# A state-space layer's y clipped and gated in eight pieces of 512 tokens instead of four of 1024

## The chip, the cores and the metric

The program runs on one core of one Trainium2 chip. The metric is the device time of one launch in microseconds. Three runs of the kernel before gave 1256.93, 1259.4 and 1264.48 us, so the median is 1259.4 us. Within a core the engines named here work side by side and wait for one another through semaphores: PE (TensorE, matrix products), DVE (VectorE), ACT (ScalarE), POOL (GpSimd) and SP, which issues DMAs.

## The reference, cut to what matters

The whole program is four transformer-like layers, each a mixer and a feed-forward part. The change is in the mixer of layer 0, a Mamba-style state-space model. Its core, with 2 batches of 1024 tokens, 256 inner channels and 16 states, is:

```
h = dA * h + (dt_t * u_t)[..., None] * B_t[:, None, :]   # one step of the scan
y = jnp.einsum('bdn,bn->bd', h, C_t)
...
y = jnp.transpose(ys, (1, 0, 2)) + x * D
y = _bound(y)                       # clip to 0..1
gate = jax.nn.silu(z)
y = _bound(y * gate)
return jnp.einsum('bld,ed->ble', y, W_out)
```

After it come the residual addition, a layer norm, a modulation and the feed-forward part of layer 0, whose inputs and hidden values are rounded to FP4 in blocks of 16 (scale by the block's largest magnitude). `Bm`, `Cm`, `dt` and `z` are computed ahead of the scan and aren't touched.

(The shapes: `B` in the kernel is 2, `S` 1024, `NTOK` 2048.)

## The kernel before, in words

Everything in layer 0 is written out by hand: five functions, one for each engine's queue, and counts of semaphores that tie them together. No scheduler reorders anything. A queue is worked off in order, so a wait holds all that stands behind it on its engine.

The 256 channels are two halves of 128 partitions (`e` = 0, 1; `ET` = 2). A batch's 1024 tokens are two pieces of `CH` = 512 (`hf` = 0, 1; `CPB` = 2). The scan therefore has the steps (batch `b`, state `n`, `e`, `hf`), with `hf` running fastest: 64 steps for a batch (`per_b`), 128 in all. For each step q: PE spreads the row of B over the partitions (`b_row`, L565), DVE multiplies it by dt*u (`multiply`, L712; every fourth step on POOL instead, L909), ACT makes the decay (L852), DVE scans (L750), POOL multiplies by the row of C (L919), and PE adds the product into one of four PSUM banks (L599), bank 4 + 2e + hf. The last state closes the four banks in the order (e0, first tokens), (e0, last tokens), (e1, first tokens), (e1, last tokens). The semaphore `acc` counts these sums. PE and POOL trail the scans: DVE reaches the end of batch b at iteration q = p + `LAG` with `LAG` = 3.

There DVE (`vector_scan`, L754 to L766) clips the batch out of PSUM into `u`, one instruction for each channel half (L758, 128x1024), then multiplies by the gate `gz` in place (L765, 128x1024). `y_step` counts these four. PE's `outputs(b, hf)` multiplies a piece of 512 tokens by W_out (L578): for each of 4 tiles of 128 tokens, both halves e are summed, 8 products, which the trace shows as 16 matmul records. Both calls wait for all of the batch's y: `YSTEP * (b + 1)`.

After batch 0 DVE rounds a weight to FP4 (`quantise_weight(2)`, L216 to L246), and goes on into batch 1's scan with two residual additions among it (`add_outputs`, L719, with the statistics L145 and L149 behind it). PE must put `outputs(0, 0)` ahead of the first row, `skip_product` and sum of batch 1. After batch 1 DVE normalises the tokens of batch 0 (L168, eight instructions), does the additions of batch 1's two pieces, each behind PE's outputs, and goes into the feed-forward part: a copy of transposed weights (L1002), six products (L1008), and `quantise_h` (L216 to L246). POOL modulates the normalised tokens of batch 0 (L1067, L1069) and computes the deviations of batch 1's pieces (L160, L162). PE, after its outputs, transposes the feed-forward weights (L1078, L1081) and runs six filler products (`keep_busy`, L1126) half-way through each end of the FP4 work.

Of the kernel before, what the change touches and what calls it, by code (L numbers as in the profile page):

```python
# [6 lines left out]
ALU = mybir.AluOpType  # L7
# [9 lines left out]
B, S = 2, 1024  # L17
# [3 lines left out]
CH = 512  # L21
NCH = NTOK // CH
TPC = CH // P
CPB = S // CH
# [4 lines left out]
ET = DI // P  # L29
# [46 lines left out]
def _program(nc, A, out, top):  # L76
# [6 lines left out]
    pe, dv, ac, gp, sp = nc.tensor, nc.vector, nc.scalar, nc.gpsimd, nc.sync  # L83
    ps = top.enter_context(nc.psum_tensor("ps", [P, 8, CH], F32))
# [6 lines left out]
    gate = sb("gate", [P, NL, 2, B, D])  # L91
# [278 lines left out]
    def layer0_mixer(ctx):  # L370
# [3 lines left out]
        gz = sb("gz", [P, ET, NTOK], ctx=ctx)  # L374
        u = sb("u", [P, ET, NTOK], ctx=ctx)
# [27 lines left out]
                                                  sem("acc"))  # L403
        y_step, y_mm = sem("y_step"), sem("y_mm")
        TAPS, SKIP, SEL, NEGA = KC, KC + ET, KC + ET + 1, KC + ET + 2
        ROWS, YSTEP = 5, 2 * ET

        DT, GZ = (ET * (NCH - 1), ET * NCH + 2), ET * NCH
        SILU_1 = float(1.0 / (1.0 + np.exp(-1.0)))
# [20 lines left out]
        def y_bank(b, hf):  # L430

            return 0 if b == B - 1 and hf else 3

        def by_gpsimd(q):
            return q % per_n == per_n - 1
# [97 lines left out]
        def tensor_scan():  # L533
# [6 lines left out]
            def skip_product(b, e, hf):  # L540

                t0 = b * S + hf * CH
                pe.wait_ge(dt_out, ET * NCH + 2)
                pe.wait_ge(l0_const, SKIP)
                if b > 0:
                    pe.wait_ge(y_step, YSTEP * (b - 1) + ET)
                pe.matmul(ps[:, 4 + e * CPB + hf, :], skip[:, e, :], u[:, e, t0:t0 + CH], start=True, stop=False)

            def c_row(k, i):
# [18 lines left out]
            def outputs(b, hf, bank3):  # L568

                bank = y_bank(b, hf)  # L570
                pe.wait_ge(y_step, YSTEP * (b + 1))
                pe.wait_ge(l0_wog, B)
                if bank == 3:
                    pe.wait_ge(*bank3)
                for t in range(TPC):
                    t0 = b * S + hf * CH + t * P
                    for e in range(ET):
                        i = pe.matmul(ps[:, bank, t * P:(t + 1) * P], u[:, e, t0:t0 + P], wog[:, b, e, :],  # L578
                                      start=e == 0, stop=e == ET - 1)
                i.then_inc(y_mm, 1)  # L580
                return x_new, b * CPB + hf + 1
# [5 lines left out]
            for q in range(NQ + LAG):  # L587
# [5 lines left out]
                p = q - LAG  # L593
# [112 lines left out]
        def vector_scan():  # L706
# [20 lines left out]
            for q in range(NQ + LAG):  # L727
                if q in add_at:
                    add_outputs(0, add_at[q])
                if q in REST_AT:  # L730
                    rest_bc(1, REST_AT[q])
                if q == 24:
                    rows_dt(1)
                if q + 1 < NQ and not by_gpsimd(q + 1):
                    multiply(q + 1)
                if q < NQ:
                    b, n, e, hf = steps[q]
                    k = q // per_n
                    if by_gpsimd(q):
                        dv.wait_ge(gp_inputs, k + 1)  # L740
                        operands = ps[:, q % NB_, :], gin[:, k % 2, :]
                    else:
                        dv.wait_ge(inputs, nth(q) + 1)
                        operands = dA[:, q % SL, :], ps[:, q % NB_, :]
                    dv.wait_ge(decayed, q + 1)
                    if q >= SL:
                        dv.wait_ge(times_c, q - SL + 1)
                    if hf:
                        dv.wait_ge(scanned, q)
                    dv.tensor_tensor_scan(hs[:, q % SL, :], *operands,  # L750
                                          hs[:, (q - 1) % SL, CH - 1:CH] if hf else 0.0,
                                          ALU.mult, ALU.add).then_inc(scanned, 1)
                p = q - LAG
                if p >= 0 and p % per_b == per_b - 1:  # L754
                    b = p // per_b
                    dv.wait_ge(acc, p + 1)
                    for e in range(ET):
                        dv.tensor_scalar(u[:, e, b * S:(b + 1) * S],  # L758
                                         ps[:, 4 + e * CPB:4 + (e + 1) * CPB, :].rearrange("p a n -> p (a n)"),
                                         0.0, 1.0, ALU.max, ALU.min).then_inc(y_step, 1)  # L760
                    dv.wait_ge(xz_z, GZ + ET * (b + 1))
                    for e in range(ET):
                        dst = u[:, e, b * S:(b + 1) * S]
                        dv.wait_ge(y_step, YSTEP * b + e + 1)
                        dv.scalar_tensor_tensor(dst, gz[:, e, b * S:(b + 1) * S], SILU_1, dst,  # L765
                                                ALU.min, ALU.mult).then_inc(y_step, 1)  # L766
                    if b == 0:
                        quantise_weight(2)
                    else:
                        for c in range(b * CPB):  # L770
                            normalise(1, c)
                        for hf in range(CPB):
                            add_outputs(b, hf)
# [2327 lines left out]
```

## Time and profile before

| what | value |
|---|---|
| median of 3 runs | 1259.4 us (1256.93 to 1264.48) |
| span of the profiled execution | 1233.1 us |
| what lies around the span, against the median | 26.3 us |
| PE busy | 908.0 us, 74% |
| DVE busy | 899.4 us, 73% |
| ACT busy | 581.5 us, 47% |
| POOL busy | 548.8 us, 45% |
| mean granted TensorE clock | 0.865 |

The profile holds no device time of its own for the execution it shows. The 26.3 us are the median less the span, and stand here for what lies before the first and after the last instruction. Layer 0's scan runs from about 80 to 316 us, its feed-forward part from there to about 425 us. In the rows a time is the start in us from the span's first instruction. One row can hold several instructions of a kind (x2), and its duration then covers them all. Where a bracket ends the row, the engine was idle for that long before it, until the named engine's instruction.

### The profile page before, as it was taken

The numbers are of one execution on the slowest core, as the hardware profiler recorded it, in microseconds if no ns is written. First come the engines' busy times: TensorE is split into PE (matmuls) and PEld (weight loads), VectorE is DVE, ScalarE is ACT, GpSimd is POOL, SyncE is SP. The second block draws the span as 40 slices with busy tenths as digits, with TensorE's granted clock in tenths as the row PEclk, the third lists the DMA queues.
The fourth block names the chain that finished last, engine by engine and source line by source line (L and its number), as shares of the span: only waits on it lengthen the run. The fifth ranks groups of instructions, "written<-read, shape, count | busy, mean of one in ns | idle before, by whom it ended". The sixth has DMA issues, their size and how long they took to land.

```text
span 1233.1 us, 18682 instructions
## 1 busy us (share of the span) xinstructions
PE 908.0 (74%) x5207; PEld 528.8 (43%) x5207; DVE 899.4 (73%) x1692; ACT 581.5 (47%) x1232; POOL 548.8 (45%) x553
## 2 busy tenths in 40 slices
PE   6977787888666676668888888858996481258992
PEld 3423233333335544212223322348996251156882
DVE  6679999999899737787888875185553689984323
ACT  3477664666033242506776667624543481023332
POOL 2058996999410132501111211225643587335753
PEclk9879898999878897959999999869998595568997
DMA  9000000000000210320110110061111000001113
GB/s 300 1 1 1 1 0 1 1 0 1 1 0 1 86 51 0 100 66 17 28 32 24 28 28 2 1 241 40 45 35 53 38 1 0 0 35 40 48 40 115
DMA packets 28016, 46.30 MB, mean 38 GB/s; under 512 B 8720, under 2 KB 16408, under 8 KB 26896
## 3 DMA queue, kind: packets, MB, share of 16 engines
q1 hardware_dynamic: 22672, 34.67, 8.7%
q0 software_dynamic: 4096, 8.35, 2.3%
q10 hardware_dynamic: 1152, 2.10, 0.5%
q8 instruction: 48, 0.79, 0.3%
q14 instruction: 48, 0.39, 0.1%
HBM read 34.46 MB, written 12.58 MB: 38 GB/s over the span
## 4 chain that ended last, share of the span: by engine, by line
PE 43%; DVE 29%; issue 11%; ACT 7%; POOL 5%; DMA 3%; SPq 1%; DVEq 0%; ACTq 0%; POOLq 0%
PE ps L2791 10%; PE ps L2800 6%; PE ps L1814 5%; PE ps L1796 4%; POOL sb_gs L919 4%; DVE sb_hs L750 3%; DVE sb_l_mxp L1928 2%; PE ps L1741 2%; DVE sb_xn L168 2%; DVE sb_stats L145 2%; ACT sb_l_rc L2221 1%; PE ps L1749 1%; PE ps L599 1%; ACT sb_l_pT L1871 1%; PE ps L478 1%
## 5 line engine op out<-in xcount | busy, mean ns | idle before, releaser
L1928 DVE TENSOR_REDUCE sb_l_mxp<-ps 128x2 f32<-128x1024 f32 (+3 forms) x152 | 171.3, 1163 | 40.1 <-PE ps L1741 38.8
L919 POOL TENSOR_TENSOR sb_gs<-sb_hs,sb_xp 128x512 f32<-128x512 f32 x128 | 163.2, 1295 | 23.7 <-DVE sb_hs L750 21.9
L1871 ACT ACTIVATE sb_l_pT<-ps 128x512 f32<-128x512 f32 (+3 forms) x256 | 111.4, 521 | 76.3 <-PE ps L1796 75.0
L599 PE MATMUL ps<-sb_gs,sb_ident 128*128 128x512 f32 x256 | 133.9, 605 | 1.0 <-POOL sb_gs L919 0.8
L2791 PE MATMUL ps<-sb_hT,sb_f_shared 128*128 x936 | 123.8, 283 | 6.5 <-issue 2.4
L2791 PEld LDWEIGHTS ps<-sb_hT,sb_f_shared 128*128 128x128 f32 x936 | 113.3, 196 | 14.9 <-issue 14.9
L1796 PE MATMUL ps<-sb_l_qk 51*128 51x512 bf16 (+3 forms) x384 | 88.6, 334 | 18.9 <-ACT sb_l_pT L1871 8.1
L2861 DVE SCALAR_TENSOR_TENSOR sb_f_rows<-ps,sb_f_mask,sb_f_rows 128x128 f32 x78 | 27.3, 351 | 91.1 <-PE ps L2800 61.3
L865 ACT ACTIVATE sb_xp<-ps 128x512 f32<-128x512 f32 x96 | 57.1, 595 | 73.2 <-POOL sb_gs L919 41.6
L2889 POOL DMA_INDIRECT moe_y<-sb_f_rows,sb_f_rowi x64 | 64.1, 1002 | 61.3 <-DVE sb_f_rows L2861 49.4
L2830 ACT ACTIVATE sb_f_hid<-ps 128x512 f32<-128x512 f32 x78 | 46.6, 597 | 90.7 <-PE ps L2791 90.7
L2800 PE MATMUL ps<-sb_sw_f_out,sb_f_hid 128*128 x624 | 83.5, 277 | 0.7 <-DVE sb_f_hid L2850 0.6
L2884 POOL DMA_INDIRECT sb_f_inq<-moe_h,sb_f_toki x64 | 62.9, 983 | 43.7 <-DVE sb_f_rowi L2662 16.3
L750 DVE TENSOR_TENSOR_SCAN sb_hs<-sb_dA,ps 128x512 f32<-128x512 f32 x64 | 76.8, 1200 | 0.1
L2800 PEld LDWEIGHTS ps<-sb_sw_f_out,sb_f_hid 128*128 128x128 f32 x624 | 75.8, 192 | 1.2 <-issue 1.1
L160 POOL TENSOR_SCALAR sb_rstd<-sb_meanvar 128x4 f32<-128x4 f32 x32 | 9.9, 311 | 146.9 <-DVE sb_meanvar L149 146.8
L1741 PE MATMUL ps<-sb_l_qk 48*128 48x128 bf16 (+3 forms) x576 | 68.3, 297 | 8.6 <-DVE sb_l_mxp L1928 8.5
L1796 PEld LDWEIGHTS ps<-sb_l_qk 51*128 51x128 bf16 x384 | 25.5, 94 | 113.4 <-issue 107.9
L2017 POOL TENSOR_SCALAR_AFFINE_SELECT sb_l_raw<-sb_l_raw 128x512 f32<-128x512 f32 x24 | 15.2, 634 | 130.7 <-ACT sb_l_raw L1871 130.6
L2017 POOL TENSOR_SCALAR_AFFINE_SELECT sb_l_pT<-sb_l_pT 128x512 f32<-128x512 f32 x40 | 25.4, 635 | 95.2 <-ACT sb_l_pT L1871 95.1
L712 DVE TENSOR_TENSOR ps<-sb_mod_space,ps 128x512 f32<-128x512 f32 x96 | 64.5, 672 | 4.1 <-PE ps L565 4.1
L852 ACT ACTIVATE sb_dA<-sb_dt,sb_negA 128x512 f32<-128x512 f32 x96 | 65.5, 712 | 0.8 <-DVE sb_hs L750 0.8
(394 smaller groups left out, 2047.1 us busy)
## 6 DMA issues: line engine op xcount, KB each, us to landing
sb_sw_f_in<-w_f_in SPq DMA_DIRECT2D x2, 2048.0 KB, 10.3
sb_sw_f_out<-w_f_out SPq DMA_DIRECT2D x2, 2048.0 KB, 13.9
sb_l_qk<-spill SPq DMA_DIRECT2D x112, 32.0 KB
spill<-sb_l_parts SPq DMA_DIRECT2D x12, 256.0 KB, 2.9
moe_y<-c_f_zero SPq DMA_DIRECT2D x1, 2048.0 KB, 9.5
sb_sw_f_up<-w_f_up SPq DMA_DIRECT2D x1, 2048.0 KB, 12.0
moe_h<-sb_f_rows SPq DMA_DIRECT2D x8, 256.0 KB, 5.2
sb_f_rows<-moe_y SPq DMA_DIRECT2D x8, 256.0 KB, 6.0
```

Source lines behind the costliest of these rows:

```text
L599: pe.matmul(ps[:, 4 + e * CPB + hf, :], ident[:], gs[:, p % SL, :], start=False, stop=n == DS - 1).then_inc(acc, 1)
L712: dv.tensor_tensor(ps[:, q % NB_, :], dtu[:, e, t0:t0 + CH], ps[:, q % NB_, :], ALU.mult).then_inc(inputs, 1)
L750: dv.tensor_tensor_scan(hs[:, q % SL, :], *operands, hs[:, (q - 1) % SL, CH - 1:CH] if hf else 0.0, ALU.mult, ALU.add).then_inc(scanned, 1)
L852: ac.activation(dst, dt[:, e, t0:t0 + CH], ACT.Exp, scale=negA[:, e, n:n + 1]).then_inc(decayed, 1)
L919: gp.tensor_tensor(gs[:, q % SL, :], hs[:, q % SL, :], cs[:, k % 2, hf * CH:(hf + 1) * CH], ALU.mult).then_inc(times_c, 1)
L1741: m = pe.matmul(ps[:, b0 + half, col:col + width], qs[i][rows, slot, t * P:(t + 1) * P], ks[i][rows, slot, key:key + width], start=start, ...
L1796: pe.matmul(ps[:, bank[n_sc], 0:width], ks[i][rows, h // 2, kt * P:(kt + 1) * P], qs[i][rows, h // 2, q0:q0 + width], start=True, stop=Tru ...
L1871: ac.activation(pT[e % 3][:, h, 0:width], ps[:, bank[n_bank], 0:width], ACT.Exp, scale=L2_SCALE).then_inc(exped, 1)
L1928: dv.tensor_reduce(dst, src, AX_X, ALU.max).then_inc(max_out, 1)
L2791: m = pe.matmul(ps[:, 2 * (i % 2) + n, fs], own[:, i % 2, n, fs], xr[:, bass.ds(r, 1), :], start=True, stop=True)
L2800: m = pe.matmul(ps[:, Y_BANK[i % 2], 0:D], hid[:, i % NBUF, f * P:(f + 1) * P], w_out[:, bass.ds(e, 1), f, :], start=f == 0, stop=f == FT - 1)
L2889: gp.indirect_dma_start(ysum, bass.IndirectOffsetOnAxis(ap=row_i[:, k:k + 1], axis=0), y_all[:, k, :], None, bounds_check=2 * NTOK - 1, oo ...
```

## The change

The clip and the gate are issued as eight instructions of 128x512 instead of four of 128x1024. Their order is a table: the clips of channel half 0 (first, last tokens), the gates of half 0, then for half 1 clip and gate of the first tokens, clip and gate of the last tokens. Each clip waits for the last sum of its own bank, each gate for its own clip. `outputs(b, hf)` waits for the gate of channel half 1 and its own tokens, which is the sixth of the eight for `hf` = 0 and the eighth for `hf` = 1. The first product into each bank of batch 1 (`skip_product`) waits for the clip of that bank. The wait for `gz` stands ahead of the clips. The line numbers below this place grow by 6 or more.

```diff
-        ROWS, YSTEP = 5, 2 * ET
+        ROWS, YSTEP = 5, 2 * ET * CPB
...
+        Y_ORDER = ([("clip", 0, hf) for hf in range(CPB)] + [("gate", 0, hf) for hf in range(CPB)]
+                   + [(what, e, hf) for hf in range(CPB) for e in range(1, ET) for what in ("clip", "gate")])
+
+        def y_at(b, what, e, hf):
+            return y_step, YSTEP * b + Y_ORDER.index((what, e, hf)) + 1
...
                 if b > 0:
-                    pe.wait_ge(y_step, YSTEP * (b - 1) + ET)
+                    pe.wait_ge(*y_at(b - 1, "clip", e, hf))
...
-                pe.wait_ge(y_step, YSTEP * (b + 1))
+                pe.wait_ge(*y_at(b, "gate", ET - 1, hf))
...
-                    dv.wait_ge(acc, p + 1)
-                    for e in range(ET):
-                        dv.tensor_scalar(u[:, e, b * S:(b + 1) * S],
-                                         ps[:, 4 + e * CPB:4 + (e + 1) * CPB, :].rearrange("p a n -> p (a n)"),
-                                         0.0, 1.0, ALU.max, ALU.min).then_inc(y_step, 1)
                     dv.wait_ge(xz_z, GZ + ET * (b + 1))
-                    for e in range(ET):
-                        dst = u[:, e, b * S:(b + 1) * S]
-                        dv.wait_ge(y_step, YSTEP * b + e + 1)
-                        dv.scalar_tensor_tensor(dst, gz[:, e, b * S:(b + 1) * S], SILU_1, dst,
-                                                ALU.min, ALU.mult).then_inc(y_step, 1)
+                    for what, e, hf in Y_ORDER:
+                        t0 = b * S + hf * CH
+                        dst = u[:, e, t0:t0 + CH]
+                        if what == "clip":
+                            dv.wait_ge(acc, p + 1 - per_n + e * CPB + hf + 1)
+                            dv.tensor_scalar(dst, ps[:, 4 + e * CPB + hf, :], 0.0, 1.0,
+                                             ALU.max, ALU.min).then_inc(y_step, 1)
+                        else:
+                            dv.wait_ge(*y_at(b, "clip", e, hf))
+                            dv.scalar_tensor_tensor(dst, gz[:, e, t0:t0 + CH], SILU_1, dst,
+                                                    ALU.min, ALU.mult).then_inc(y_step, 1)
```

DVE's queue at the end of batch 1, before: the last scan, then the clips of whole halves out of the banks `ps`, the gates, and the first normalisation. The brackets name the semaphores that an instruction waits for.

```order
L750 SCALAR_TENSOR_TENSOR sb_hs<-ps,sb_hs,sb_xp 128x512 [waits times_c,scanned,decayed,gp_inputs]
L758 TENSOR_SCALAR sb_u<-ps 128x1024 [waits acc]
L758 TENSOR_SCALAR sb_u<-ps 128x1024
L765 SCALAR_TENSOR_TENSOR sb_u<-sb_gz,sb_u 128x1024 [waits y_step,xz_z]
L765 SCALAR_TENSOR_TENSOR sb_u<-sb_gz,sb_u 128x1024 [waits y_step]
L168 TENSOR_SCALAR sb_xn<-sb_x,sb_meanvar,sb_rstd 128x128 [waits ln_rstd]
```

The same place of the changed kernel:

```order
L756 SCALAR_TENSOR_TENSOR sb_hs<-ps,sb_hs,sb_xp 128x512 [waits times_c,scanned,decayed,gp_inputs]
L768 TENSOR_SCALAR sb_u<-ps 128x512 [waits acc,xz_z]
L768 TENSOR_SCALAR sb_u<-ps 128x512 [waits acc]
L772 SCALAR_TENSOR_TENSOR sb_u<-sb_gz,sb_u 128x512 [waits y_step] x2
L768 TENSOR_SCALAR sb_u<-ps 128x512 [waits acc]
L772 SCALAR_TENSOR_TENSOR sb_u<-sb_gz,sb_u 128x512 [waits y_step]
L768 TENSOR_SCALAR sb_u<-ps 128x512 [waits acc]
L772 SCALAR_TENSOR_TENSOR sb_u<-sb_gz,sb_u 128x512 [waits y_step]
L168 TENSOR_SCALAR sb_xn<-sb_x,sb_meanvar,sb_rstd 128x128 [waits ln_rstd]
```

The four instructions have become eight, and every clip has its own wait for `acc`. Nothing else on DVE has changed its place. The end of batch 0 has the same eight, between the scan of step 66 and `quantise_weight(2)`.

PE's queue is the same before and after, but for the counts it waits for. It is shown at the end of batch 0, where three things of batch 1 stand behind the first outputs (L578): the row of B (L565), the product that opens a bank (L547) and the first sum (L599). Then come the outputs of the last tokens.

```order
L599 MATMUL ps<-sb_gs,sb_ident 128x512 [waits times_c]
L578 MATMUL ps<-sb_wog,sb_u 128x128 [waits crow,l0_wog,y_step]
L578 MATMUL ps<-sb_wog,sb_u 128x128 x7
L565 MATMUL ps<-sb_bc,sb_sel 128x512 [waits scanned,rows_step]
L547 MATMUL ps<-sb_u,sb_skip 128x512 [waits y_step,l0_const,dt_out]
L599 MATMUL ps<-sb_gs,sb_ident 128x512 [waits times_c]
L578 MATMUL ps<-sb_wog,sb_u 128x128 [waits x_new,l0_wog,y_step]
L578 MATMUL ps<-sb_wog,sb_u 128x128 x7
```

No row moves here. What moves is the time at which `y_step` lets the first L578 go.

## Rows read from the trace of the kernel before

**Rows 1.** Busy time by stretch: start:end, length, PE, PEld, DVE, ACT, POOL, clock, DMA, GB/s.
```profile
218.00:308.00 90.00, 73.40 (x195) 28.35 (x194) 87.92 (x97) 57.96 (x97) 86.84 (x73) 0.98 0.00 1
329.80:417.80 88.00, 54.82 (x212) 37.29 (x213) 84.92 (x135) 23.63 (x65) 11.21 (x12) 0.78 0.00 1
```

**Rows 2.** DVE in order of time, end of batch 0: start, us, instruction.
```profile
199.47 1.19 DVE L750 TENSOR_TENSOR_SCAN sb_hs<-sb_dA,ps 128x512 f32<-128x512 f32 x1
201.19 2.35 DVE L758 TENSOR_SCALAR sb_u<-ps 128x1024 f32<-128x1024 f32 x2 [0.52 <-PE ps L599]
203.46 2.35 DVE L765 SCALAR_TENSOR_TENSOR sb_u<-sb_gz,sb_u 128x1024 f32<-128x1024 f32 x2
205.73 0.51 DVE L216 TENSOR_REDUCE sb_f0w_small<-sb_sw_f_dn 128x22 f32<-128x352 f32 x1
...
209.90 0.68 DVE L719 TENSOR_TENSOR sb_x<-sb_x,ps 128x512 f32<-128x512 f32 x1
...
212.40 1.27 DVE L750 TENSOR_TENSOR_SCAN sb_hs<-ps,sb_hs,sb_xp 128x512 f32<-128x512 f32 x1
214.21 0.69 DVE L719 TENSOR_TENSOR sb_x<-sb_x,ps 128x512 f32<-128x512 f32 x1 [0.54 <-PE ps L578]
```

**Rows 3.** DVE in order of time, end of batch 1 and start of the feed-forward part.
```profile
307.60 0.67 DVE L712 TENSOR_TENSOR ps<-sb_mod_space,ps 128x512 f32<-128x512 f32 x1
308.18 1.21 DVE L750 TENSOR_TENSOR_SCAN sb_hs<-sb_dA,ps 128x512 f32<-128x512 f32 x1
...
312.41 1.28 DVE L750 TENSOR_TENSOR_SCAN sb_hs<-ps,sb_hs,sb_xp 128x512 f32<-128x512 f32 x1
316.36 2.35 DVE L758 TENSOR_SCALAR sb_u<-ps 128x1024 f32<-128x1024 f32 x2 [2.67 <-PE ps L599]
318.63 2.35 DVE L765 SCALAR_TENSOR_TENSOR sb_u<-sb_gz,sb_u 128x1024 f32<-128x1024 f32 x2
320.90 2.13 DVE L168 TENSOR_SCALAR sb_xn<-sb_x,sb_meanvar,sb_rstd 128x128 f32<-128x128 f32 x8
324.86 0.69 DVE L719 TENSOR_TENSOR sb_x<-sb_x,ps 128x512 f32<-128x512 f32 x1 [1.82 <-PE ps L578]
...
327.84 0.69 DVE L719 TENSOR_TENSOR sb_x<-sb_x,ps 128x512 f32<-128x512 f32 x1 [0.97 <-PE ps L578]
...
329.76 0.86 DVE L1002 COPY sb_f_wguT<-ps 128x704 f32<-128x704 f32 x1
```

**Rows 4.** PE in order of time, around both ends.
```profile
212.22 1.95 PE L578 MATMUL ps<-sb_wog,sb_u 128*128 128x128 f32 x16
...
311.54 4.79 PE L599 MATMUL ps<-sb_gs,sb_ident 128*128 128x512 f32 x8 [0.75 <-POOL sb_gs L919]
321.04 6.76 PE L578 MATMUL ps<-sb_wog,sb_u 128*128 128x128 f32 x32 [4.71 <-DVE sb_u L765]
```

**Rows 5.** One form on DVE, 128x512 with two inputs in SBUF (L624).
```profile
L624 DVE SCALAR_TENSOR_TENSOR sb_u<-sb_xp,sb_sw_l_vec,sb_u x12: 750/752/753, 22.2 to 35.9; 128x512 f32<-128x512 f32 x12
```

**Rows 6.** POOL in order of time, at both ends and in the feed-forward part.
```profile
198.61 3.73 POOL L919 TENSOR_TENSOR sb_gs<-sb_hs,sb_xp 128x512 f32<-128x512 f32 x3
...
310.22 4.93 POOL L919 TENSOR_TENSOR sb_gs<-sb_hs,sb_xp 128x512 f32<-128x512 f32 x4
...
328.59 1.04 POOL L162 TENSOR_TENSOR sb_rstd<-sb_rstd,sb_half 128x4 f32<-128x4 f32 x1
...
341.74 1.28 POOL L1067 TENSOR_TENSOR sb_hT<-sb_xn,sb_mod 128x512 f32<-128x512 f32 x1
```

**Rows 7.** DVE, the same step of the FP4 work, twice.
```profile
333.25 0.69 DVE L228 TENSOR_TENSOR sb_f_tmp<-sb_hT,sb_f_small 128x512 f32<-128x512 f32 x1
...
341.87 1.70 DVE L228 TENSOR_TENSOR sb_f_tmp<-sb_hT,sb_f_small 128x512 f32<-128x512 f32 x1
```

**Rows 8.** Busy time by stretch around the ends, and later.
```profile
201.20:205.80 4.60, 0.00 (x0) 0.00 (x0) 4.60 (x5) 0.94 (x2) 1.14 (x1) 0.84 0.00 0
205.80:211.20 5.40, 5.34 (x19) 4.53 (x20) 5.05 (x15) 0.00 (x0) 0.00 (x0) 0.51 0.00 0
316.30:321.00 4.70, 0.03 (x1) 0.00 (x0) 4.64 (x5) 0.00 (x0) 0.00 (x0) 0.93 0.01 2
321.00:327.30 6.30, 6.26 (x29) 6.26 (x30) 3.97 (x17) 0.00 (x0) 4.03 (x4) 0.51 0.00 0
415.00:419.30 4.30, 4.25 (x19) 3.83 (x20) 2.80 (x13) 1.50 (x6) 1.26 (x2) 0.50 0.00 0
421.80:460.00 38.20, 28.15 (x132) 18.56 (x130) 15.51 (x56) 19.07 (x28) 13.47 (x12) 1.00 0.28 110
```

## The prediction

> **What bounds the kernel now.** I read the views in this order: busy time by stretch, to see which engine has no room near the change. Then DVE in order of time at the two places where a batch ends, then PE and POOL at the same places, and last the clock. In the body of the scan DVE is busy for 87.92 of 90 us and POOL for 86.84 [rows 1]. So anything that DVE saves or loses at the end of batch 0 is passed on unshortened. In the feed-forward part behind the scan DVE is busy for 84.92 of 88 us [rows 1], and the reader should see that it is the engine with the least room up to 416 us. A microsecond gained by DVE at 329.76 is a microsecond gained at the end of layer 0's feed-forward part.
>
> At the end of batch 0 DVE finishes its scan at 199.47 + 1.19 = 200.66, and starts to clip at 201.19, behind PE's last sum. It then works without a hole until 213.67, and waits 0.54 us for PE's second outputs [rows 2]. At the end of batch 1 there is more to see. DVE's last scan ends at 312.41 + 1.28 = 313.69. The four last sums are one chain on PE from 311.54 to 316.33 [rows 4], paced by POOL, whose four products run from 310.22 to 315.15 [rows 6]. DVE idles 2.67 us and clips at 316.36 when the last is in [rows 3]. Its gates end at 320.98, PE starts the outputs at 321.04 after 4.71 us without work [rows 4], and DVE, having normalised, waits for them 1.82 us and then 0.97 us [rows 3]. These three holes, 5.46 us, are what could be won there. The second pair is PE's time: 32 matmul records in 6.76 us [rows 4] at a granted clock of 0.51 [rows 8], the lower level of 1.2 GHz. The same 16 records took 1.95 us at full clock [rows 4].
>
> **The change part by part.**
>
> The eight pieces. A whole clip or gate starts 2.27/2 = 1.135 us after the one before it (201.19, 203.46, 205.73) [rows 2]. A 128x512 instruction on DVE starts 0.58 us before the next (307.60 to 308.18 [rows 3]), while its own duration is 0.67. Eight at 0.58 are 4.64 us against 4.54 before. Two gates stand right behind the clip they wait for (half 1), so each pays a full duration and a little, about 0.14 more: 4.64 + 0.28 = 4.92, taken as 4.95. Bounds: 4.64 from below, and 8 x 0.75 = 6.0 from above, if every piece costs what L624 costs [rows 5]. I take 4.95, nearest to the row of the same shape without a scalar from memory. The cost is +0.4 us a batch.
>
> POOL beside the gates. The gates read two tensors from SBUF, and now start while POOL still multiplies. The trace has such a meeting: the same DVE step took 0.69 us alone, and 1.70 us when it began at 341.87 within POOL's 341.74 to 343.02 [rows 6, 7]. It ended at 343.57, which is POOL's end plus about its own time, so it was held until POOL had finished. By these rows a gate that starts while POOL works is held to the end of that POOL instruction. At batch 0 the first gate would start at about 201.8, and POOL works to 202.34 [rows 6]: +0.5 us. At batch 1 it would start at about 314.8, and POOL's last product ends at 315.15: +0.35 us. The bounds are 0 and these values. I take them in full. The Trainium skill's page "SBUF — State Buffer", section "SBUF: two separate sides", has this as a lock: a DVE instruction with two SBUF inputs and a GpSimd instruction that reads SBUF exclude each other for a whole instruction. By the page the two delays are what the rows give, and without it the sum would be 0.85 us better.
>
> Batch 0 then: the clips start 0.59 us earlier (200.60, as a follower starts 0.08 before the end of the one ahead), the pieces take 0.41 more, the lock 0.5. DVE is 0.3 us later at L216. PE's first outputs wait for the sixth piece, at about 200.60 + 4 x 0.58 + 0.5 + 0.72 + 0.67 = 204.8, and start 1.0 us earlier than 205.86 even at the low clock. So the row, the opening product and the sum of batch 1 that stand behind them on PE are earlier too, and the second outputs are bound by DVE's first addition instead (209.90 [rows 2] + 0.3 + 0.69 = 210.9). They take 1.95 us, and are ready at 212.9, before DVE's scan ends at 213.97. The 0.54 us hole goes. Batch 0: -0.2 us.
>
> Batch 1: the first clip starts at 313.61 right behind the scan (its bank's sum, the first of four in 4.79 us [rows 4], is over by 312.8). The clip of (half 1, first tokens) comes at 313.61 + 2.32 + 0.35 = 316.28, its sum, the third, ends a sum and a wait, 1.2 us, before 316.33. The last clip's sum ends at 316.33, before DVE asks for it at 317.6. No clip waits. The gates end with DVE free at 313.61 + 4.95 + 0.35 = 318.91, against 320.90: -2.0 us. PE may start its outputs at the end of the sixth piece, 317.7, instead of 321.04, after only 1.4 us without work. In the scan PE has holes of that kind all the time at a clock of 0.98 [rows 1]. The clock fell before, late in a hole of 4.7 us (mean 0.93 in 316.3 to 321.0 [rows 8]). So I take the full clock: 16 records in 1.95 us, the first outputs ready at 319.7, the second at 321.6. DVE normalises until 320.97, adds at once, and comes to the second addition 2.0 us later, at 323.0. Both holes go: -1.82 - 0.97 = -2.79. Batch 1: -4.8 us at L1002, which would start at 325.0.
>
> What is late next. The weights' transposes on PE end near 323, before DVE asks. POOL's modulations follow the normalisation and end near 326.4. Only then do its two deviations come, each with an instruction of 1.04 us [rows 6], and they now lie beside DVE's FP4 steps from 327, where before they lay beside additions and copies that read PSUM. If they hold DVE once, that costs up to 0.8 us. The trace doesn't show this pair. Bounds 0 and 0.8, and I take the middle, 0.4, having no nearer row.
>
> Behind that everything is shifted together up to 416 us, where the end of layer 0 and all later stages follow. Sum: -0.2 - 4.8 + 0.4 = -4.6 us. The profiled execution has a span of 1233.1 us, and 26.3 us lie between that and the median: 1228.5 + 26.3 = 1254.8 us (-0.37%).
>
> **The rivals.**
>
> Rival 1, the clock stays low for the outputs. At batch 0 it had fallen by 205.8, and was at 0.51 until 211.2 [rows 8]. If PE's outputs of batch 1 run at the lower level, 32 records take about 6.8 us. From 317.7 the first 16 end at 321.5 and the second at 324.9, so 0.55 + 1.4 = 2.0 us of DVE's holes stay. Gain 2.6 us, time 1256.8. Against it stands the short hole of 1.4 us.
>
> Rival 2, more than the sum. If POOL doesn't hold the gates or the FP4 steps, 0.85 + 0.4 us come back. The chain at the end of the feed-forward part (415.0 to 419.3 at a clock of 0.50, PE busy for 4.25 of 4.3 us [rows 8]) can fall at full clock once it comes at another moment, worth up to 4.3/2 = 2.1 us. Together 3.4 more: 1251.4. For it: the clock's spells are not tied to the kernel's stages. Against: the rows of POOL and DVE are plain.
>
> Rival 3, slower: low-clock spells move into stages that PE bounds. From 421.8 to 460 PE is busy 28.15 of 38.2 us at a clock of 1.00 [rows 8]. A spell like the one of 321 to 327.3 there would cost 6.3 x 0.74 / 2 = 2.3 us. Everything behind 318 us comes 4.8 us earlier, so where spells fall is dealt anew. Two more such spells take the gain back, and from there it is slower. With four it is 1254.8 + 9.2 = 1264.0. For it: the mean clock is 0.865, so much is at stake. Against: the low spells of today can go as well as come, and four more of one sign are unlikely.
>
> Rival 4, the gain doesn't last: the feed-forward part turns out to wait for PE or POOL, whose work doesn't come earlier. Then only batch 0's 0.2 us stays, 1259.2. DVE's 84.92 of 88 us [rows 1] speaks against it.
>
> **How the numbers follow.** The forecast gets 0.50 (own range 1252.5 to 1257), rival 1 0.12, rival 2 0.22, rival 3 0.12, rival 4 0.04. Half a per cent of 1259.4 is 6.3 us, about what a measurement can tell from no change. So faster means below 1253.1: rival 2 and a tail of the forecast, 0.30. Slower means above 1265.7, the upper tail of rival 3, 0.07. The rest, 0.63, is within. The range goes from 1248.5, a little beyond rival 2, to 1260.5, which takes in rivals 1 and 4 and a part of rival 3. The likeliest time is faster than before, but by less than can be told with certainty.
>
> **What would show each step.** Right: eight rows of 128x512 at each end, about 0.67 us each with starts 0.58 apart. The first gate longer than the second by about 0.5 us at batch 0 and 0.35 at batch 1. No idle time before L768 at batch 1 (2.67 before). L584, the outputs, after a hole of about 1.4 us at clock 1.0, 16 records in 1.95 us. No hole before either L725 at batch 1. The copy of the weights (L1002 before) 4.8 + 0.2 = 5.0 us earlier. Wrong: a clip that still waits for PE, pieces near 0.75 us, or outputs at 0.5. The forecast as a whole is wrong if the last gates of layer 0 are 5 us earlier and the span isn't.

## The result and the profile after

Over 20 runs of each kernel the changed one had a median of 1258.74 us, against 1263.2 us of the kernel before. The medians are 4.5 us apart. The ratio is 0.9953, with a 95% interval of 0.9935 to 0.9971: 5.9 us less, 3.7 to 8.2. One run of the changed kernel took 1407.42 us at a granted clock of 0.62 and is left out of the ratio. So the changed kernel is faster, by a little less than half a per cent, the outcome to which the prediction gave 0.63. Two later measurements beside the experiments gave 0.9944 (0.9923 to 0.9966) and 0.9959 (0.9941 to 0.9977). The forecast was -4.6 us, 1254.8 us, with a range of 1248.5 to 1260.5.

The profiled execution of the changed kernel has a span of 1257.2 us and took 1258.5 us. So only 1.3 us lie around this span, and not the 26.3 us that the first table and the forecast took for it. The first experiment below says what those were.

DVE at the end of batch 0, to be read against [rows 2]; the columns are start, duration, engine, line, operation and operands.

```profile
198.84 1.19 DVE L756 TENSOR_TENSOR_SCAN sb_hs<-sb_dA,ps 128x512 f32<-128x512 f32 x1
199.96 1.26 DVE L768 TENSOR_SCALAR sb_u<-ps 128x512 f32<-128x512 f32 x2
201.13 1.72 DVE L772 SCALAR_TENSOR_TENSOR sb_u<-sb_gz,sb_u 128x512 f32<-128x512 f32 x2
202.78 0.68 DVE L768 TENSOR_SCALAR sb_u<-ps 128x512 f32<-128x512 f32 x1
203.49 0.69 DVE L772 SCALAR_TENSOR_TENSOR sb_u<-sb_gz,sb_u 128x512 f32<-128x512 f32 x1
...
205.43 0.51 DVE L216 TENSOR_REDUCE sb_f0w_small<-sb_sw_f_dn 128x22 f32<-128x352 f32 x1
...
213.29 0.66 DVE L725 TENSOR_TENSOR sb_x<-sb_x,ps 128x512 f32<-128x512 f32 x1
```

The scan of step 66 started 0.63 us earlier than in the first profile, for a cause ahead of the change, so ways are compared and not clock times. From the start of that scan to the start of the second addition it is 213.29 - 198.84 = 14.45 us, against 14.74. The addition has no idle time before it now. Batch 0 gives 0.29 us.

DVE at the end of batch 1, against [rows 3]:

```profile
311.47 1.28 DVE L756 TENSOR_TENSOR_SCAN sb_hs<-ps,sb_hs,sb_xp 128x512 f32<-128x512 f32 x1
312.67 1.26 DVE L768 TENSOR_SCALAR sb_u<-ps 128x512 f32<-128x512 f32 x2
313.85 1.50 DVE L772 SCALAR_TENSOR_TENSOR sb_u<-sb_gz,sb_u 128x512 f32<-128x512 f32 x2
315.28 0.68 DVE L768 TENSOR_SCALAR sb_u<-ps 128x512 f32<-128x512 f32 x1
315.99 0.69 DVE L772 SCALAR_TENSOR_TENSOR sb_u<-sb_gz,sb_u 128x512 f32<-128x512 f32 x1
316.60 0.68 DVE L768 TENSOR_SCALAR sb_u<-ps 128x512 f32<-128x512 f32 x1
317.31 0.69 DVE L772 SCALAR_TENSOR_TENSOR sb_u<-sb_gz,sb_u 128x512 f32<-128x512 f32 x1
317.92 2.14 DVE L168 TENSOR_SCALAR sb_xn<-sb_x,sb_meanvar,sb_rstd 128x128 f32<-128x128 f32 x8
319.98 0.68 DVE L725 TENSOR_TENSOR sb_x<-sb_x,ps 128x512 f32<-128x512 f32 x1
...
321.89 0.66 DVE L725 TENSOR_TENSOR sb_x<-sb_x,ps 128x512 f32<-128x512 f32 x1
...
323.79 0.86 DVE L1009 COPY sb_f_wguT<-ps 128x704 f32<-128x704 f32 x1
```

No row has idle time before it: 2.67, 1.82 and 0.97 us are gone. From the start of the last scan to the copy of the weights it is 12.32 us, against 17.35. That is 5.03 us, the whole of batch 1's gain. I call this way "the batch 1 way" below, and the 14.45 us "the batch 0 way".

PE at the same place, against [rows 4]:

```profile
310.59 4.79 PE L605 MATMUL ps<-sb_gs,sb_ident 128*128 128x512 f32 x8 [0.75 <-POOL sb_gs L926]
316.73 3.84 PE L584 MATMUL ps<-sb_wog,sb_u 128*128 128x128 f32 x32 [1.35 <-DVE sb_u L772]
```

The 32 records take 3.84 us instead of 6.76, behind a hole of 1.35 instead of 4.71. Busy time by stretch says why (length, PE, PEld, DVE, ACT, POOL, then the granted clock):

```profile
316.70:320.60 3.90, 3.87 (x34) 3.87 (x35) 3.87 (x11) 0.00 (x0) 0.46 (x1) 1.00 0.01 2
...
411.10:417.60 6.50, 4.99 (x35) 3.92 (x33) 3.76 (x18) 2.97 (x8) 2.43 (x5) 1.00 0.17 35
```

The clock is 1.00 in the outputs, the level of 2.4 GHz, where it was 0.51. The second row is the tail of the feed-forward part. There the last piece's chain ran at 1.00, where [rows 8] show 0.50 for most of it. DVE's rows there:

```profile
410.83 1.09 DVE L168 TENSOR_SCALAR sb_xn<-sb_x,sb_meanvar,sb_rstd 128x128 f32<-128x128 f32 x4
414.12 0.69 DVE L1040 TENSOR_TENSOR sb_x<-sb_x,ps 128x512 f32<-128x512 f32 x1 [2.20 <-PE ps L1125]
...
417.60 2.13 DVE L168 TENSOR_SCALAR sb_xn<-sb_x,sb_meanvar,sb_rstd 128x128 f32<-128x128 f32 x4 [0.47 <-POOL sb_rstd L162]
```

DVE waits 2.20 us for PE there. The same view of the kernel before has a longer wait at this addition:

```profile
421.75 0.69 DVE L1033 TENSOR_TENSOR sb_x<-sb_x,ps 128x512 f32<-128x512 f32 x1 [3.89 <-PE ps L1118]
```

So another 1.7 us were gained at a place that the change doesn't touch. There the granted clock was at 0.50 from 409.1 to 419.4 us before, and from 401.5 to 408.3 us in the changed kernel, ahead of this chain. This 1.7 us does not come each time: it was there in two of three profiles of the changed kernel and in three other kernels' profiles, one of which has batch 1 as before. In the third profile of the changed kernel the wait was 3.79 us.

POOL and DVE in the feed-forward part, where 0.4 us of holding was forecast. First POOL, then DVE:

```profile
325.60 1.07 POOL L162 TENSOR_TENSOR sb_rstd<-sb_rstd,sb_half 128x4 f32<-128x4 f32 x1
...
326.93 1.04 POOL L162 TENSOR_TENSOR sb_rstd<-sb_rstd,sb_half 128x4 f32<-128x4 f32 x1
```

```profile
326.46 0.18 DVE L219 TENSOR_SCALAR sb_f_small<-sb_f_small 128x32 f32<-128x32 f32 x1
...
327.27 0.69 DVE L228 TENSOR_TENSOR sb_f_tmp<-sb_hT,sb_f_small 128x512 f32<-128x512 f32 x1
```

Both DVE steps began within a POOL instruction of about 1.04 us and took what they take alone. The second is the very step (L228) that took 1.70 us beside a 128x512 instruction of POOL in [rows 7]. Nothing was held. The kernel before has the same kind of pair, further on in the feed-forward part, POOL first and then DVE:

```profile
401.45 1.04 POOL L162 TENSOR_TENSOR sb_rstd<-sb_rstd,sb_half 128x4 f32<-128x4 f32 x1
```

```profile
401.97 1.61 DVE L1028 TENSOR_TENSOR sb_f_hh<-sb_f_sg 128x1408 f32<-128x1408 f32 x1
```

This DVE step too has two inputs in SBUF. It began half-way through the POOL instruction and took 1.61 us, like its three repetitions elsewhere (1.59 to 1.62).

### The profile page after: what moved, and what is told of

It is laid out like the page before. It is cut to its first block, busy times and chain, and to the rows that moved or that the text cites. A ratio compares the mean times of both kernels' runs of the same rounds, so it can differ in the third digit from the quotient of the medians.

```text
span 1257.2 us, 18690 instructions
## 1 busy us (share of the span) xinstructions
PE 915.5 (73%) x5207; PEld 533.2 (42%) x5207; DVE 899.7 (72%) x1700; ACT 578.6 (46%) x1232; POOL 547.4 (44%) x553
## 4 chain that ended last, share of the span: by engine, by line
PE 39%; DVE 30%; issue 11%; ACT 8%; POOL 5%; DMA 3%; another core or an unknown queue 2%; SPq 1%; DVEq 0%; ACTq 0%; POOLq 0%
PE ps L2798 9%; PE ps L2807 5%; PE ps L1821 5%; PE ps L1803 4%; DVE sb_hs L756 3%; POOL sb_gs L926 3%; DVE sb_l_mxp L1935 2%; PE ps L1748 2%; DVE sb_xn L168 2%; DVE sb_stats L145 2%; ACT sb_l_rc L2228 1%; PE ps L1756 1%; ACT sb_l_pT L1878 1%; DVE ps L718 1%
## 5 line engine op out<-in xcount | busy, mean ns | idle before, releaser
L2798 PE MATMUL ps<-sb_hT,sb_f_shared 128*128 x936 | 127.5, 288 | 13.6 <-ACT sb_f_shared L2815 6.8
L2798 PEld LDWEIGHTS ps<-sb_hT,sb_f_shared 128*128 128x128 f32 x936 | 116.6, 200 | 22.2 <-issue 22.2
L2807 PE MATMUL ps<-sb_sw_f_out,sb_f_hid 128*128 x624 | 86.3, 283 | 14.0 <-ACT sb_f_hid L2837 9.3
L2807 PEld LDWEIGHTS ps<-sb_sw_f_out,sb_f_hid 128*128 128x128 f32 x624 | 78.6, 198 | 15.9 <-issue 15.7
```

The costliest lines, as they stand in the source:

```text
L2798: m = pe.matmul(ps[:, 2 * (i % 2) + n, fs], own[:, i % 2, n, fs], xr[:, bass.ds(r, 1), :], start=True, stop=True)
L2807: m = pe.matmul(ps[:, Y_BANK[i % 2], 0:D], hid[:, i % NBUF, f * P:(f + 1) * P], w_out[:, bass.ds(e, 1), f, :], start=f == 0, stop=f == FT - 1)
```

## The experiments

Each variant was timed in 7 to 12 executions beside 29 to 35 of the kernel before. That settles a time to 2 to 3 us. The ways in the profile repeat to 0.01 to 0.06 us between the profiles of one kernel, and they decide here. Between different kernels the same instructions can differ by more, where a spell of low clock falls elsewhere: two such cases, of 0.6 and 1.2 us, are below. The ways also leave out what lies around them. The scan of step 66 starts between 196.1 and 201.6 us in the fourteen profiles. From the second addition of batch 0 to the last scan it is 98.2 us in most of them, but 97.0 in the third profile of the changed kernel, since one low-clock spell of PE in the scan isn't there.

**The kernel before, again.** No edit.

> The kernel before, once more, to see what span and what profile it has on the same chip as the experiments. If the profile shown before (span 1233.1 us) was of an ordinary execution, this one's span lies near 1233 too and its reported time is some 26 us above it. If that execution was an unusual one, which lacked stalls behind 840 us that others have, then this span is about 1258 to 1262, some 1.3 us below its time, and the last 400 us show waits as the changed kernel's profile has them. Local times up to 330 us should agree with the first profile within about 1 us.

Its ratio to itself came out as 0.998 (0.9952 to 1.0008), which shows how much such a ratio is worth. The span was 1257.3 us, 2.1 us below its time, and the ways 14.68 and 17.31 us. So the second case holds: the profile of the kernel before, with its span of 1233.1 us, was of an execution without some 24 us of stalls. Some 23 of them lie in the mixture-of-experts stages of the last two layers. Here are the first profile, the repeated one and the third profile of the changed kernel, each with the stretches between the same instructions of DVE. The first profile:

```profile
841.00:897.00 56.00, 56.00 (x503) 55.80 (x502) 29.90 (x74) 28.35 (x63) 33.19 (x34) 1.00 0.14 40
1104.00:1188.00 84.00, 72.57 (x534) 61.85 (x535) 35.84 (x115) 27.87 (x64) 54.25 (x54) 0.92 0.14 42
```

The kernel before, repeated:

```profile
843.40:907.00 63.60, 59.63 (x518) 57.76 (x516) 28.86 (x74) 27.09 (x62) 33.70 (x34) 1.00 0.13 37
1114.00:1213.30 99.30, 76.95 (x542) 67.20 (x542) 35.51 (x115) 26.77 (x64) 53.26 (x55) 0.88 0.12 36
```

The changed kernel, third measurement:

```profile
836.10:892.20 56.10, 56.10 (x504) 55.90 (x502) 30.15 (x74) 28.37 (x63) 33.04 (x34) 1.00 0.14 40
1099.80:1183.50 83.70, 72.80 (x536) 62.15 (x537) 35.52 (x114) 27.47 (x64) 54.35 (x54) 0.92 0.14 42
```

The first stretch takes 56.0, 63.6 and 56.1 us, the second 84.0, 99.3 and 83.7. In the last of the three jobs the kernel before had a median of 1237.37 us, in the first two of 1259.6 and 1260.08. All four profiles of the last job have the short stretches, all eight of the first two jobs the long ones. The first two jobs ran on one chip, the last on another, so the 24 us don't go with the kernel. They go with the chip or with the job: only one job ran on the second chip, and for the first profile of either kernel the chip isn't on record. In the long ones the chain of waits names a releaser that the profile can't see. What it is stays open. The comparisons are within one job and aren't touched.

**Batch 1 alone.** Batch 0 keeps its four instructions, which count for two each in `y_step`.

```diff
-                    for what, e, hf in Y_ORDER:
+                    if b == 0:
...
+                    for what, e, hf in (Y_ORDER if b != 0 else []):
```

> Eight pieces for batch 1 alone; batch 0 clipped and gated in four instructions of 1024 tokens as before. Theory (the gain is made at batch 1, by DVE's early start and PE's shorter hole): the way from the last scan's start to the copy of the feed-forward weights is 12.3 us as in the changed kernel, against 17.35 before; at batch 0 the second addition waits 0.5 us for PE again. Time 0.3 us above the changed kernel, about 5.0 us below before. Rival (batch 0 makes a good part of it by moving the clock's spells): less than 3 us below before.

The batch 1 way was 326.45 - 314.14 = 12.31 us, as in the changed kernel, and the hole before the second addition of batch 0 was back (1.00 us). The batch 0 way was 15.29 us, 0.6 us more than in the kernel before with the same instructions: here PE's clock stayed low until 213.3 us, over the products ahead of that addition. The time was 1254.32 us, ratio 0.9961 (0.9935 to 0.9987), -4.9 us. The end of the feed-forward part had the 1.7 us as well (a wait of 2.21 us), so at the start of layer 1, counted from the scan of step 66, this kernel was 6.1 us ahead of the one before. Batch 1 makes 5.0 of the 5.3 us of the two ways.

**Batch 0 alone.** The same with the batches exchanged.

> Eight pieces for batch 0 alone; batch 1 as before. Theory: only the hole before the second addition (0.54 us) and the early start (0.5 us) go, against 0.4 us more of instructions and 0.46 us of holding by POOL: 0.2 to 0.3 us below before, no difference that can be measured; the way from batch 1's last scan to the weights' copy is 17.3 us again. Rival: 2 us or more below before.

The batch 0 way was 14.44 us, 0.3 us less than before. The batch 1 way was 16.10 us instead of 17.35, with the same instructions in it. The row of PE says how:

```profile
321.12 5.31 PE L586 MATMUL ps<-sb_wog,sb_u 128*128 128x128 f32 x32 [4.81 <-DVE sb_u L774]
```

The outputs took 5.31 us instead of 6.76 since the low-clock spell ended earlier in them, at 324.2 us instead of 327.2. The ratio was 0.9973 (0.9951 to 0.9995), -3.4 us with an interval from -6.2 to -0.6. The 1.5 us of the two ways are in it, and so are 1.7 us at the end of the feed-forward part, where DVE waited 2.21 us for PE instead of 3.89. Together that is 3.2 us at layer 1. So in this profile the rival's 2 us or more were there, by the places where the low clock fell and not by the eight pieces themselves. The interval of the time ends at -0.6, so the 0.2 to 0.3 us of the theory lie just outside it.

**Outputs wait for all eight.**

```diff
-                pe.wait_ge(*y_at(b, "gate", ET - 1, hf))
+                pe.wait_ge(y_step, YSTEP * (b + 1))
```

> The changed kernel, but PE's outputs of both pieces wait for all eight. DVE's pieces start as early as in the changed kernel. PE's hole at batch 1 grows from 1.35 to 2.7 us; the first outputs start at the last gate's end, 1.3 us later. If the clock stays full (the hole is short), the first outputs are ready 1.3 us later, at about the end of the normalisation, so DVE has no hole or one under 0.2 us: the same time as the changed kernel within 0.3 us. The outputs' own early start would then be worth nothing, and DVE's early start all. If the clock falls in the 2.7 us hole, the outputs take 6.8 us instead of 3.8 and DVE waits 2 to 3 us: time 2 to 3 us above the changed kernel.

PE's row, and the two additions of DVE:

```profile
316.73 5.47 PE L584 MATMUL ps<-sb_wog,sb_u 128*128 128x128 f32 x32 [2.67 <-DVE sb_u L772]
```

```profile
319.40 0.69 DVE L725 TENSOR_TENSOR sb_x<-sb_x,ps 128x512 f32<-128x512 f32 x1 [0.67 <-PE ps L584]
...
322.24 0.69 DVE L725 TENSOR_TENSOR sb_x<-sb_x,ps 128x512 f32<-128x512 f32 x1 [0.83 <-PE ps L584]
```

The batch 1 way was 14.02 us, 1.7 more than the changed kernel's. Neither branch of the expectation was quite right. The clock did fall, but late: it was at 1.00 through the hole and until 318.0 us, 1.3 us into the outputs, then at 0.50 until 321.5. The outputs took 5.47 us. So in this run the clock fell behind a hole of 2.67 us, and the early start of the outputs is worth 1.7 us by way of the clock. At batch 0 PE's hole was 5.04 us and the way 15.00 us, with a wait of 0.48 us before the second addition. The time was 1255.81 us (0.9964, 0.994 to 0.9987).

**Eight pieces, all behind the last sum.**

```diff
-                            dv.wait_ge(acc, p + 1 - per_n + e * CPB + hf + 1)
+                            dv.wait_ge(acc, p + 1)
```

> The changed kernel, but every clip waits for the batch's last sum, as before: eight pieces without the early start. Theory (sum of the terms): DVE clips from 316.3 instead of 313.6 at batch 1, so 2.7 us of the gain go, less the 0.24 us that POOL no longer holds the gates; PE's hole at batch 1 grows to 3.6 us (4 pieces, a clip and a gate after the last sum). With the clock still full the outputs stay hidden, and the way from last scan to weights' copy is 12.3 + 2.4 = 14.7 us; the time is 2.5 us above the changed kernel. If the clock falls in that hole, it is 16.5 to 17 us and nothing is left of the gain. Rival (the early start is worthless since PE's outputs were the bound): no difference to the changed kernel.

```profile
315.23 1.29 DVE L768 TENSOR_SCALAR sb_u<-ps 128x512 f32<-128x512 f32 x2 [2.73 <-PE ps L605]
316.43 1.28 DVE L772 SCALAR_TENSOR_TENSOR sb_u<-sb_gz,sb_u 128x512 f32<-128x512 f32 x2
```

The hole of 2.7 us is back, and the two first gates take 1.28 us instead of 1.50, since POOL has ended. The batch 1 way was 15.31 us, 3.0 more than the changed kernel's, against 2.4 expected, and the batch 0 way 14.70 us. The rest is a PE hole of 3.98 us with the outputs at 5.46 us, and a wait of 0.21 us before the second addition. The time was 1257.97 us (0.9976, 0.9956 to 0.9996), against 0.9944 of the changed kernel in the same job. The rival, that the early start is worthless, falls by the way; the two intervals of the time just overlap.

**All clips, then all gates.**

```diff
-        Y_ORDER = ([("clip", 0, hf) for hf in range(CPB)] + [("gate", 0, hf) for hf in range(CPB)]
-                   + [(what, e, hf) for hf in range(CPB) for e in range(1, ET) for what in ("clip", "gate")])
+        Y_ORDER = [(what, e, hf) for what in ("clip", "gate") for e in range(ET) for hf in range(CPB)]
```

> The changed kernel with the eight in another order: all four clips, then all four gates (channel half 0 first). If POOL's multiplication is what holds the first gate, then at batch 0 the gates start after POOL's last product and each takes 0.68 us: the eight take 0.46 us less. At batch 1 the clips wait for the last sum, and the gates end about 0.6 us later than in the changed kernel; PE starts 1 us later. If the long first gate has another cause (its dependence on the clip, or its position), the first gate is long here as well. Time within 0.5 us of the changed kernel, not to be told apart.

```profile
201.64 2.45 DVE L767 TENSOR_SCALAR sb_u<-ps 128x512 f32<-128x512 f32 x4
204.01 2.48 DVE L771 SCALAR_TENSOR_TENSOR sb_u<-sb_gz,sb_u 128x512 f32<-128x512 f32 x4
```

No gate is long here: POOL's concurrent product was what held the first one. The eight take 4.85 us instead of 5.55 (199.96 to 204.82 + 0.69). Of the 0.70 us, 0.46 are the hold (1.72 against 1.26 for two), and the rest are the two gates that no longer stand right behind their clips. The batch 0 way was 13.74 us. At batch 1 the last two clips waited 0.27 and 0.54 us for their sums, PE's hole was 2.59 us (outputs 5.46 us) and the way 13.93 us, 1.6 longer. Time 1256.0 us (0.9964, 0.9944 to 0.9985).

**The kernel before with a shorter hole on PE.**

```diff
                 bank = y_bank(b, hf)
+                if b == B - 1 and hf == 0:
+                    pe.wait_ge(scanned, NQ)
+                    for _ in range(4):
+                        pe.matmul(ps[:, 2, :], ident[:], gs[:, 0, :], start=True, stop=True)
                 pe.wait_ge(y_step, YSTEP * (b + 1))
```

> The kernel before with four more products of 128x512 on PE into an unused bank, between batch 1's last sum and its first outputs, so that PE's hole there shrinks from 4.7 to about 1.3 us. It parts the gain at batch 1 into what the clock gives and what DVE's early start gives. Theory: the outputs run at full clock as in the changed kernel (3.84 us for both instead of 6.76); they still start at the last gate's end, so the first addition comes at the end of the normalisation and neither addition waits: the way from the last scan to the weights' copy is 17.35 - 1.82 - 0.97 = 14.6 us, against 12.3 of the changed kernel. So 2.8 us of 5.0 are the clock's holes, 2.2 are DVE's early start less its longer pieces. Rival (the hole isn't what lowers the clock): 17.3 us again, and the outputs at half clock.

```profile
317.64 3.84 PE L582 MATMUL ps<-sb_wog,sb_u 128*128 128x128 f32 x32 [1.28 <-DVE sb_u L769]
```

```profile
309.02 1.28 DVE L754 TENSOR_TENSOR_SCAN sb_hs<-ps,sb_hs,sb_xp 128x512 f32<-128x512 f32 x1
...
319.73 0.69 DVE L723 TENSOR_TENSOR sb_x<-sb_x,ps 128x512 f32<-128x512 f32 x1
321.66 0.66 DVE L723 TENSOR_TENSOR sb_x<-sb_x,ps 128x512 f32<-128x512 f32 x1
...
323.55 0.86 DVE L1006 COPY sb_f_wguT<-ps 128x704 f32<-128x704 f32 x1
```

The way was 14.53 us, as expected (14.6), with four products that compute nothing (the trace shows them as 8 records in 3.60 us; in the same way the six of `keep_busy` are three products). So of the 5.0 us of the batch 1 way, 2.8 are the clock's, and 2.2 are DVE's early start less its longer pieces. But the time did not follow: 1237.56 us against 1237.37, ratio 1.001 (0.9992 to 1.0028). A gain of 2.8 us is outside that interval, though at layer 1 the profile still has this kernel 3.0 us ahead of the one before, so what was lost lies behind. In its profile the stretch between the start of layer 1 and the middle of layer 2's attention took more than in the first profile. This kernel first, then the kernel before:

```profile
470.60:680.60 210.00, 164.00 (x1170) 58.02 (x1173) 163.18 (x232) 109.13 (x242) 42.47 (x57) 0.85 0.15 40
```

```profile
475.80:680.30 204.50, 159.58 (x1177) 57.86 (x1181) 162.85 (x233) 109.44 (x243) 42.49 (x57) 0.87 0.15 41
```

5.5 us more for the same work, with a lower granted clock. This is one profile each, and the same stretch took 207.9 us in the repeated kernel before and 206.1, 206.5 and 204.6 us in the three profiles of the changed one. So it may be what rival 3 described, at a smaller scale, but it isn't shown that this swallowed the gain.

**The changed kernel again**, in the second and the third job.

> The changed kernel once more, timed beside the variants of this job. About 5 us below before (ratio 0.996). Its profile repeats the local times: 5.0 us less from the last scan to the weights' copy, the first two gates of each batch held by POOL.

> The changed kernel a third time, beside the last variants. Ratio to before 0.994 to 0.997; local times as before: 14.45 us at batch 0, 12.3 us at batch 1.

Ratios 0.9944 and 0.9959, 1252.46 and 1231.97 us. The batch 1 way was 12.31 and 12.32 us, the batch 0 way 14.44 and 14.46.

**Batch 0 with all clips first, batch 1 as changed.** `y_order(b)` gives the one order for batch 0 and the other for batch 1.

> The changed kernel, with batch 0's eight in the order all clips, then all gates, and batch 1's as in the changed kernel. From the run with that order at both ends: the way from the scan of step 66 to the second addition is 13.7 us instead of 14.45 at batch 0, and at batch 1 the way to the weights' copy stays 12.3 us. 0.7 us below the changed kernel, not to be told apart by time.

The ways were 13.77 and 12.31 us, as expected. The time was 1230.98 us (0.9945, 0.9925 to 0.9965), against 1231.97 of the changed kernel in the same job. Of the orders of the eight pieces it is the best by its ways, and it can't be told from the changed kernel by time.

**The lower clips on ACT.** ACT does max(y, 0) out of PSUM, DVE one min(y, 1) times the gate. The upper clip of the gate is made by a second activation, S - relu(S - g).

```diff
+                        ac.wait_ge(acc, p + 1 - per_n + e * CPB + hf + 1)
+                        ac.activation(u[:, e, t0:t0 + CH], ps[:, 4 + e * CPB + hf, :], ACT.Relu).then_inc(y_relu, 1)
...
+                            dv.wait_ge(y_relu, per_n * b + e * CPB + hf + 1)
+                            dv.scalar_tensor_tensor(dst, dst, 1.0, gz[:, e, t0:t0 + CH],
+                                                    ALU.min, ALU.mult).then_inc(y_step, 1)
```

> A version meant to beat both: ACT, which is idle for over 12 us at both ends, takes the lower clip (Relu out of PSUM, four of 128x512 a batch, behind each bank's last sum), and DVE does only min(y, 1) times the gate, four of 128x512 a batch. The upper clip of the gate moves to ACT too (a second activation of 128x1024 beside each of the four that are there). Theory: DVE is the engine without room, so batch 0 wins 4 x 0.6 = 2.4 us, less if ACT's pieces come late; at batch 1 the last gate can't end before the last sum (0.3 us after 316) + ACT 0.6 + DVE 0.7, about 1 us before the changed kernel's. Together 3 us below the changed kernel, 8 below before. Rival: the four additional ACT instructions (1.05 us each) or ACT's wait for the sums hold up the decays, and the gain is lost in the scan: no better than the changed kernel.

> The version with the lower clips on ACT once more, beside the changed kernel. Its local gain was 1.45 us at batch 0 and 0.8 us at batch 1, its time 1256.05 us against 1252.46 of the changed kernel in that job. If the later stages' spread hid the gain, it is now 1 to 3 us below the changed kernel; if something later in the program really costs, it is above it again.

In both jobs the ways were shorter: 12.99 and 13.01 us at batch 0, 11.50 at batch 1, together 2.3 us less than the changed kernel. The times were 1256.05 us (0.996, 0.9937 to 0.9984) and 1232.7 us (0.9963, 0.9942 to 0.9983). Both points lie above the changed kernel's of the same job, by 3.6 and 0.7 us, though the intervals overlap. The expected further 3 us did not come. At layer 1 the two profiles are 1.5 to 2.6 us ahead of the changed kernel's three, counted from the scan of step 66. Whether the extra activations cost time ahead of that scan, or the clock's spells behind layer 1 do, two profiles don't tell.

## Why the prediction was right, step by step

- The eight pieces: 0.59 us apart and 0.68 long, as forecast (0.58 and 0.67). A gate right behind its clip starts 0.71 us after it (0.72 forecast). Their sum with the hold was 5.47 us at batch 0, against 5.45.
- POOL's hold: two gates in 1.72 and 1.50 us, against 1.26 without it. That is 0.46 and 0.24 us, where 0.5 and 0.35 were forecast. The order with the clips first and the one behind the last sum take it away. The lock that the Trainium skill states in "SBUF — State Buffer", section "SBUF: two separate sides", agrees with this pair. It does not fit the 128x4 pair three items below: there POOL's instruction reads SBUF too, and a DVE step with two SBUF inputs was not held. The measurement decides.
- Batch 0: -0.29 us against -0.2.
- Batch 1: -5.03 us against -4.8. The start at once behind the scan, the hole of 1.35 us (1.4), the full clock and the two vanished waits all came as said. The filler experiment shows that the clock is 2.8 us of it, more than half. It shows that for the way and not for the time, which stayed the same.
- The hold of FP4 steps by POOL's 128x4 instructions: 0, where 0.4 was put in the middle of 0 to 0.8. This term was mis-sized. The prediction says that the trace doesn't show this pair. It does: the rows at 401.45 and 401.97 us of the kernel before, shown above, are such a pair and put the term at 0. With it at 0 the sum would have been -5.0, and the two ways measured give -5.3.
- The passing on: DVE's lead of 5.3 us reached the end of the feed-forward part whole, and was 7 us at layer 1, by 1.7 us of the tail at full clock. That is the second half of rival 2, priced there at up to 2.1. It came in two of three profiles of the changed kernel, and the sum had it at nothing.
- What was wrong is the bridge from span to time. The 26.3 us are 1 to 3 us around the span and some 24 us of stalls that the first profile lacks. It didn't harm the forecast, which by this sum is the first median less 4.6 us. The measured 1258.74 us is 3.9 us above it, and nearly all of that is the first median: over 20 runs the kernel before had 1263.2 us, 3.8 more than over the first three. How near the difference came, 4.5 or 5.9 us against 4.6, is partly luck. The profile's lead at layer 1 was 7.0 us, and from the start of layer 1 on, outside the two long stretches, the three profiles of the changed kernel took 665.2, 667.5 and 670.0 us.
- Rival 1 (low clock in the outputs) did not happen in the change, but in all variants with holes of 2.6 us and more ahead of the outputs the clock fell. Rival 4 falls. Rival 3's mechanism, spells dealt anew, was seen in the gaining direction (1.7 us) and in the losing one (0.6 us at batch 0 of the kernel with batch 1 alone), and may stand behind the 5.5 us of the filler's profile. Why local gains of 2 to 3 us (the filler, ACT's clips) were not found again in the time is not settled.

## What to carry to other kernels

When a serial end of a stage is cut into pieces, look at the engine that idles meanwhile: here more than half of the gain of the batch 1 way came from TensorE keeping its clock, since its hole shrank from 4.7 to 1.35 us, and behind one of 2.7 us the clock fell. Compare ways between two instructions of one engine, not clock times or spans; they repeat to 0.05 us where the run's time spreads by several. But see what lies around a way as well: part of what the whole program gained or lost was elsewhere, and a local gain of 2.8 us was not found in the time. Before a span is set against a median, see that both come from the same chip and the same job. Before a term is called one that the trace doesn't show, look for its pair of instructions in the whole trace.

## What the runs showed of the hardware that was not expected

- The same two stretches took 56 and 84 us in five profiles, and 61 to 66 and 98 to 103 us in nine, some 23 us of the 24 by which the spans differ. The eight profiles of the two jobs on one chip are all long, the four of the one job on another all short.
- A POOL instruction of 128x4 and 1.04 us (the power at L162) held no DVE step that began within it: L228 took 0.69 us there. One of 128x512 held the same step until its own end, 1.70 us [rows 6, 7], and with one input too DVE was held there: L219, at 333.8 us of the changed kernel, took 0.76 us beside a 128x512 instruction, and 0.18 us beside the 128x4 one.
- Ahead of batch 1's outputs the clock fell within holes of PE of 4.71 and 4.81 us, 0.3 to 0.7 us before their end (outputs of 6.76, 6.74 and 5.31 us). Behind holes of 3.98, 2.67 and 2.59 us it fell only 0.6 to 1.3 us into the outputs (5.46, 5.47 and 5.46 us). It did not fall in or behind holes of 1.28, 1.35 and 1.36 us (3.84 us). The length of the hole alone doesn't decide: 4.71 and 4.81 us gave 6.76 and 5.31 us, and behind the same hole of 2.10 us in batch 1's scan, with the same work, the clock fell in the first profile of the changed kernel and not in the third.
